# Output product of the biased layers split six and two, and the written-out order replaced

## The chip, the cores and the metric

One core of one Trainium2 chip runs the whole program. The metric is device time in microseconds (us) of one execution; the kernel before was timed in three runs.

## The reference, cut to what matters

Eight sequences (B = 8) of 512 tokens (T), width 256 (D), go through four layers, each with a layer norm ahead of it and a residual sum behind it:

```
x = x + attn_a(layernorm(x))     # l = 0: causal attention, 16 heads of 16, rotary positions
x = x + ffn(layernorm(x))        # l = 1: gate picks the top 256 of 512 tokens, attention among them
x = x + attn_b(layernorm(x))     # l = 2: attention, 16 heads of 64, learned relative bias
x = x + ffn(layernorm(x))        # l = 3: as l = 1
```

The change is in attn_b. Its last lines are, for each sequence:

```
attn = softmax(q @ k.T * 64**-0.5 + bias)
out = (attn @ v).transpose(0, 2, 1, 3).reshape(b, t, 16 * 64)
return out @ w_out.T                      # (512, 1024) by (1024, 256)
```

## The kernel before

**Steps.** The program is cut into steps `Step(kind, s, l, n, q)`: `s` is the sequence, `l` the layer, `n` and `q` count parts. Kinds that begin with `c_` belong to the causal layer, `f_` to the gated layers, `b_` to the biased layer. A step owns one or more of the eight PSUM banks (`UNITS`, with the engine that empties each), some matmuls on TensorE (PE), and the work behind them on VectorE (DVE), ScalarE (ACT), GpSimd (POOL) and the SP queue.

**The biased layer** handles heads in eight pairs `n`. For a pair: `b_k`, `b_q`, `b_v` project (each 1 bank); `b_row` (4 for a pair, one for each 128 tokens) makes scores of both heads in two banks, to which DVE adds the bias and takes maxima, ACT the exponentials; `b_nrm` divides on POOL; `b_tr` turns the rows around on PE and ACT copies them out; `b_val` (4 parts into one bank) multiplies by the values, and behind its last part DVE copies the bank to `OTb[:, n, :]` (line 1561). When the pairs are done, `b_y` multiplies by `wob`: `b_y(0, .)` for tokens 0 to 255 and `b_y(1, .)` for tokens 256 to 511, each in two parts `q` that add up in one bank: pairs 0 to 3, then pairs 4 to 7, 16 matmuls a part (line 1603). Behind `q = 1` DVE adds the bank to `x`, takes the moments for the next layer norm, and SP stores the rows.

**Where the steps of a kind run in the array.** Most kinds use all 128 rows and columns of PE. `c_p1`, `c_p2`, `f_p1`, `f_p2` (scores with heads of 16) use 32 rows, four heads at once; `b_row` uses 64 rows; `b_val` 64 columns; `c_va`, `c_vb`, `f_va`, `f_vb` 32 columns. The kernel's planner names these groups in `TILES`.

**Order.** Every engine walks one list, `plan.order`, and takes from it what is its own; waits are on semaphores whose counts follow from the list. The list comes from `in_order`: of all steps whose predecessors are listed, the one with the lowest `turn` goes next.

```
def turn(x):
    row, cycle = stage(x)
    return PLACE[row, x.kind][x.n * SEVERAL.get(x.kind, 1) + x.q] + CYCLE * cycle
```

`PLACE` is a table written out by hand or by a search, with the rows `first`, `first0`, `first1` (start), `cycle` and `cycle3` (six cycles that repeat for sequences 1 to 6, `CYCLE = 2820` apart), `last`, `last1`, `last2` (end). In one cycle the biased layer of sequence s runs among the causal layer and the first gated layer of s+1 and the last gated layer of s-1. `causal_steps`, `ffn_steps` and `biased_steps` list for each step what it needs and what it has to follow. `in_order` also keeps a clock of its own from the costs in `WORK`, with which it hands out banks; where that clock sees PE wait long enough, PE is given dummy transposes of the identity (line 1623).

**Steps of the last gated layer that the prediction follows.** `f_ln` (norm and gate logits), `f_row`, `f_rank` (the rank of each token: PE, then DVE writes `pick`, line 1507), `f_idx` (the token numbers, which need `pick`), `f_get` (POOL fetches the chosen rows by an indirect DMA, line 1214), `f_turn` (PE turns them around, line 1730), `f_k`, `f_q`, `f_v`, four `f_p1` (scores, DVE takes maxima, line 1533), `f_m`, four `f_p2` (scores again, less the maxima; ACT takes exponentials, line 1318), `f_va`, `f_vb`, `f_sc`, `f_add`.

Of the kernel before, what the change touches and what calls it, by code (L numbers as in the profile page):

```python
# [211 lines left out]
def wait_for(x, y):  # L212
# [52 lines left out]
    ("cycle", "f_k"): [170],
    ("cycle", "f_ln"): [-107],
    ("cycle", "f_m"): [365, 436],
    ("cycle", "f_o"): [569],
    ("cycle", "f_p1"): [320, -294, 345, 356],
    ("cycle", "f_p2"): [380, 425, 396, 262],  # L270
    ("cycle", "f_part"): [-4486],
    ("cycle", "f_q"): [184],
    ("cycle", "f_rank"): [40],
    ("cycle", "f_row"): [-1],
    ("cycle", "f_rq"): [-408],
    ("cycle", "f_spread"): [94],
    ("cycle", "f_v"): [219],
    ("cycle", "f_va"): [462, 518],
    ("cycle", "f_vb"): [-753, 405],
# [14 lines left out]
    ("cycle3", "f_q"): [5074],
    ("cycle3", "f_rank"): [4768],
    ("cycle3", "f_row"): [3336],
    ("cycle3", "f_rq"): [-1587],
    ("cycle3", "f_sc"): [5430],
# [1 line left out]
    ("cycle3", "f_v"): [5084],  # L300
    ("cycle3", "f_va"): [5264, 5321],
    ("cycle3", "f_vb"): [1319, 2872],
    ("cycle3", "f_xq"): [5131],
    ("first", "b_k"): [1394, 819, 1448, 733, 2071, 2459, 2798, 2934],
    ("first", "b_ln"): [1262],
    ("first", "b_nrm"): [1675, 401, 1780, -186, 1853, 324, 1822, 1309, 1850, 1318, 2266, 740, 2121, 1561, 2466, 2454,
        2590, 2321, 2692, 839, 2622, 1876, 2813, 2022, 2534, 3050, 3092, 3092, 2734, 2438, 3412, 3380],
    ("first", "b_q"): [292, 1680, 1268, 1633, 1493, 2254, 2809, 822],
    ("first", "b_row"): [1647, 1319, 1588, 563, 1806, 699, 882, 795, 2047, 1253, 1700, 1970, -80, -674, 2388, 2207,
        2680, 872, 2421, 2044, 2206, 2207, 2887, 2223, 2683, 3072, 2821, 3056, 1550, 2977, 3152, 3113],  # L310
    ("first", "b_tr"): [1760, 1445, 1875, 1948, 1118, 1745, 1969, 1940, 2270, 2311, 2340, 533, 2512, 1426, 923, 2494,
        2828, 2729, 2877, 2796, 2895, 2428, 2970, 3039, 3149, 3038, 3380, 3330, 3138, 3401, 3380, 3401],
# [9 lines left out]
    ("first0", "c_k"): [42, 95],
    ("first0", "c_ln"): [-178],
    ("first0", "c_m"): [400, 563],
    ("first0", "c_p1"): [238, 237, -199, 284, -197, -1423, -1423, 323, 252, 428, 323, 275],
    ("first0", "c_p2"): [292, -1395, 390, -1165, 310, 402, 399, 632, 284, -1207, 710, -954],
    ("first0", "c_q"): [30, 44],
    ("first0", "c_rq"): [-1391, 276],
    ("first0", "c_v"): [199, 145],
    ("first0", "c_va"): [529, 274, -486, 682, 724, 622],  # L330
    ("first0", "c_vb"): [585, 401, 607, 794, 720, 320],
    ("first0", "c_xq"): [111, 195],
    ("first0", "c_xt"): [17286],
    ("first0", "c_y"): [820, 273],
    ("first0", "f_gate"): [850],
    ("first0", "f_gather"): [1043],
    ("first0", "f_hk"): [752],
    ("first0", "f_hm"): [674, 1321],
    ("first0", "f_k"): [905],
    ("first0", "f_ln"): [840],  # L340
    ("first0", "f_m"): [1234, 1332],
    ("first0", "f_o"): [1437],
    ("first0", "f_p1"): [1153, 1192, 1270, 1240],
    ("first0", "f_p2"): [1293, 1250, 927, 660],
    ("first0", "f_part"): [887],
    ("first0", "f_q"): [819],
    ("first0", "f_rank"): [985],
    ("first0", "f_row"): [900],
    ("first0", "f_rq"): [-1182],
    ("first0", "f_spread"): [1430],  # L350
    ("first0", "f_v"): [1134],
    ("first0", "f_va"): [1338, 883],
    ("first0", "f_vb"): [1293, 1410],
    ("first0", "f_xq"): [1093],
    ("first0", "f_y"): [1457, 886],
    ("first1", "c_dk"): [408, 735],
    ("first1", "c_dq"): [351, 565],
    ("first1", "c_hk"): [429, 722],
    ("first1", "c_hm"): [854, 838],
    ("first1", "c_k"): [188, 278],  # L360
# [1565 lines left out]
```

How the kernel before makes its waits and increments, by code:

```python
            def at_least(engine, s, value):  # L1060
                if value > reached.get((id(engine), s.num), 0):
                    reached[id(engine), s.num] = value
                    engine.wait_ge(s, value)
# [32 lines left out]
                @block.sync  # L1097
# [10 lines left out]
                        sp.dma_start(dst[:], src).then_inc(w_rest, 16)  # L1108
                    for i in range(2):
                        sp.dma_start(wb[:, i], w_b[i]).then_inc(wb_loaded[i], 16)
                        sp.dma_start(band[:, i], band_in[i]).then_inc(band_loaded[i], 16)
                    load_x(sp, 2)
                    for now in plan.order:
                        kind, s, l, n, q = now
                        m = memory(now)
                        k = PAIRS * s + n
                        if kind == "f_vb" and l == 1 and n == 1 and 1 <= s < B - 1:
                            sp.wait_ge(heads_done, plan.after("heads", now, now))
                            load_rope(sp, s + 1)
                        if kind == "b_row" and q == NT - 1 and k + 2 < pairs:
                            sp.wait_ge(dve_read, plan.unit(now, now, "o2"))
                            sp.dma_start(band[:, k % 2], band_in[(k + 2) % PAIRS]).then_inc(band_loaded[k % 2], 16)
                        if kind == "b_v" and k + 2 < pairs:
                            sp.wait_ge(act_full, plan.unit(now, now))
                            sp.dma_start(wb[:, k % 2], w_b[(k + 2) % PAIRS]).then_inc(wb_loaded[k % 2], 16)
```

## Time and profile before

| | |
|---|---|
| median of three runs | 2005.87 us (2005.8 to 2006.48) |
| the profiled execution | 2006.36 us, its span 2004.6 us |
| PE busy | 1950.8 us, 97% of the span |
| DVE busy | 1486.9 us, 74% |
| ACT busy | 1152.3 us, 57% |
| POOL busy | 714.4 us, 36% |

Busy time of PE includes the dummy transposes and the filling and emptying of the array between matmuls of different shape. The chain that ended last is PE for 80% and DVE for 11% of its length.

### The profile page before, as it was taken

The numbers are of one execution on the slowest core, as the hardware profiler recorded it, in microseconds if no ns is written. First come the engines' busy times: TensorE is split into PE (matmuls) and PEld (weight loads), VectorE is DVE, ScalarE is ACT, GpSimd is POOL, SyncE is SP. The second block draws the span as 40 slices with busy tenths as digits, with TensorE's granted clock in tenths as the row PEclk, the third lists the DMA queues.
The fourth block names the chain that finished last, engine by engine and source line by source line (L and its number), as shares of the span: only waits on it lengthen the run. The fifth ranks groups of instructions, "written<-read, shape, count | busy, mean of one in ns | idle before, by whom it ended". The sixth has DMA issues, their size and how long they took to land.

```text
span 2004.6 us, 41582 instructions
## 1 busy us (share of the span) xinstructions
PE 1950.8 (97%) x15743; PEld 1244.9 (62%) x15743; DVE 1486.9 (74%) x4786; ACT 1152.3 (57%) x2588; POOL 714.4 (36%) x897
## 2 busy tenths in 40 slices
PE   8999999999999999999999999999999999999998
PEld 6666665656665666655666565665667556666566
DVE  8987666767879668877688677796877967856535
ACT  2554665475636766377553766457473675626753
POOL 5322324233433334333334333343333333404322
PEclk9999999999999999999999999999999999999999
DMA  4001211221201212112111122111220121212200
GB/s 171 2 2 43 72 64 45 66 69 44 76 23 62 75 41 69 38 46 98 41 56 46 36 90 59 38 47 52 80 68 26 62 69 33 76 34 81 71 12 12
DMA packets 37749, 110.02 MB, mean 55 GB/s; under 512 B 3696, under 2 KB 17648, under 8 KB 37424
## 3 DMA queue, kind: packets, MB, share of 16 engines
q1 hardware_dynamic: 34576, 103.43, 15.6%
q0 software_dynamic: 2976, 3.93, 1.1%
q8 instruction: 127, 2.08, 0.5%
q14 instruction: 70, 0.57, 0.1%
HBM read 97.39 MB, written 9.96 MB: 54 GB/s over the span
## 4 chain that ended last, share of the span: by engine, by line
PE 80%; DVE 11%; ACT 4%; issue 2%; DMA 2%; POOL 1%; POOLq 0%; DVEq 0%; ACTq 0%
PE ps L1036 24%; PE ps L1845 11%; PE ps L1837 10%; PE ps L1855 9%; PE ps L1603 9%; DVE peaks L1533 4%; PE ps L1797 3%; DVE ps L1448 3%; PE ps L1700 3%; PE ps L1686 3%; PE ps L1785 2%; ACT PTc L1294 2%; PE ps L1662 2%; DMA xg<-kept,tokens 2%; PE ps L1763 1%
## 5 line engine op out<-in xcount | busy, mean ns | idle before, releaser
L1228 POOL TENSOR_SCALAR probs<-probs,rtotal 128x512 f32<-128x512 f32 x512 | 359.2, 734 | 483.4 <-DVE rtotal L1559 483.4
L1338 ACT ACTIVATE probs<-probs,peak 128x512 f32<-128x512 f32 x512 | 365.0, 714 | 194.7 <-DVE peak L1555 194.6
L1550 DVE CUSTOM_DVE_ANT_0 probs<-ps,band 128x512 f32<-128x512 f32 x512 | 332.6, 687 | 60.8 <-PE ps L1837 60.7
L1347 ACT ACTIVATE PT<-ps 128x512 f32<-128x512 f32 x512 | 265.7, 621 | 48.8 <-PE ps L1845 48.0
L1845 PE MATMUL ps<-ident,probs 128*128 128x128 f32 x2048 | 250.3, 274 | 3.7 <-DVE peaks L1448 3.1
L1845 PEld LDWEIGHTS ps<-ident,probs 128*128 128x128 f32 x2048 | 225.8, 141 | 45.0 <-issue 34.1
L1448 DVE CUSTOM_DVE_ANT_0 ps<-ps,later 128x512 f32<-128x512 f32 (+3 forms) x512 | 232.8, 525 | 19.7 <-PE ps L1662 19.2
L1837 PE MATMUL ps<-KT,QT 64*128 64x512 f32 x1024 | 244.3, 608 | 0.0
L1855 PE MATMUL ps<-PT,Vb 128*64 128x512 f32 x1024 | 241.1, 602 | 0.0
L1036 PE MATMUL ps<-xnT,wb 128*128 128x512 f32 x512 | 234.7, 599 | 1.3 <-ACT xnT L1257 0.6
L1294 ACT ACTIVATE PTc<-ps 128x384 f32<-128x384 f32 (+1 forms) x384 | 168.0, 552 | 61.1 <-PE ps L1686 59.8
L1533 DVE TENSOR_REDUCE peaks<-ps 128x2 f32<-128x512 f32 x256 | 157.0, 682 | 26.0 <-PE ps L1763 26.0
L1036 PEld LDWEIGHTS ps<-xnT,wb 128*128 128x128 f32 x512 | 93.2, 190 | 109.5 <-issue 99.3
L1837 PEld LDWEIGHTS ps<-KT,QT 64*128 64x128 f32 x1024 | 97.6, 186 | 92.8 <-issue 71.1
L1318 ACT ACTIVATE PTf<-ps 128x512 f32<-128x512 f32 x256 | 130.2, 652 | 43.7 <-PE ps L1785 43.7
L1855 PEld LDWEIGHTS ps<-PT,Vb 128*64 128x64 f32 x1024 | 64.8, 136 | 123.3 <-issue 99.1
L1207 POOL TENSOR_SCALAR_AFFINE_SELECT PTc<-PTc 128x512 f32<-128x512 f32 x128 | 81.4, 648 | 159.3 <-ACT PTc L1294 159.3
L1036 PEld LDWEIGHTS ps<-wb,xnT 128*128 128x128 f32 x1024 | 120.6, 192 | 20.6 <-issue 9.2
L1036 PE MATMUL ps<-wb,xnT 128*128 128x128 f32 x1024 | 128.0, 279 | 0.0
L1176 POOL TENSOR_TENSOR rstd<-veps,pow_half 128x2 f32<-128x2 f32 x64 | 49.3, 800 | 185.8 <-DVE veps L1369 185.3
L1603 PE MATMUL ps<-wob,OTb 128*128 128x256 f32 x512 | 114.2, 380 | 0.5 <-DVE peaks L1448 0.5
L1603 PEld LDWEIGHTS ps<-wob,OTb 128*128 128x128 f32 x512 | 96.1, 190 | 16.9 <-issue 2.4
(191 smaller groups left out, 3213.9 us busy)
## 6 DMA issues: line engine op xcount, KB each, us to landing
band<-in_band SPq DMA_DIRECT2D x64, 896.0 KB, 4.6
wb<-in_w_b SPq DMA_DIRECT2D x64, 384.0 KB, 3.0
x<-in_x SPq DMA_DIRECT2D x16, 256.0 KB, 4.7
out<-x SPq DMA_DIRECT2D x16, 256.0 KB, 2.2
kept<-xn SPq DMA_DIRECT2D x7, 512.0 KB, 5.0
cos<-in_cos SPq DMA_DIRECT2D x8, 256.0 KB, 2.7
sin<-in_sin SPq DMA_DIRECT2D x8, 256.0 KB, 3.1
wob<-in_wo_b SPq DMA_DIRECT2D x1, 1024.0 KB, 8.5
```

The costliest lines, as they stand in the source:

```text
L1036: last = nc.tensor.matmul(o, w, r, start=(i == 0), stop=(i == len(pairs) - 1))
L1228: last = g.tensor_scalar(unit, unit, rtotal[:, r % 8, e:e + 1], 1.0, ALU.mult, ALU.mult)
L1294: a.activation(pt_c(m, q)[:, h], bank(now, name)[:, 0:w], ACT.Exp, scale=float(DH) ** -0.5).then_inc(act_read, 1)
L1338: last = a.activation(unit, unit, ACT.Exp, bias=peak[:, r % 8, e:e + 1], accum_out=total[:, r % 8, e:e + 1])
L1347: a.activation(PT[:, k % 2, e, :, tile_of(q)], bank(now, name).rearrange("p (k n) -> p k n", k=NT), ACT.Copy).then_inc(act_read, 1)
L1448: last = v.tensor_tensor_reduce(out=scores, in0=scores, in1=later[:, NT * P - w:NT * P], scale=1.0, scalar=-3e38, op0=ALU.add, op1=ALU.max ...
L1533: v.tensor_reduce(places[:, h:h + 1].rearrange("p h t -> p (h t)"), bank(now, name).rearrange("p (t n) -> p t n", t=NS), AXIS.X, ALU.max). ...
L1550: v.tensor_tensor_reduce(out=probs[:, (r + LENT) % ROWS_HELD, e, :], in0=bank(now, name), in1=band[:, k % 2, e, lo:lo + T], scale=1.0, sca ...
L1603: last = te.matmul(o[:, j * D:(j + 1) * D], w, r, start=(k == 0 and j == 0), stop=(k == count - 1 and j == 1))
L1837: full(te.matmul(bank(now, name), QT2[half(e), k % 2, tile_of(q)], KT2[half(e), k % 2, :], start=True, stop=True), now, name)
L1845: last = te.transpose(bank(now, name)[:, tile_of(t)], probs[:, (r + LENT) % ROWS_HELD, e, tile_of(t)], ident[:])
L1855: last = te.matmul(o[half(e), :], Vb[:, k % 3, q, half(e)], PT[:, k % 2, e, q, :], start=(q == 0), stop=(q == NT - 1))
```

## The change

`b_y(i, 0)` now covers pairs 0 to 5 (24 matmuls) and needs only `b_val(5, 3)`; `b_y(i, 1)` covers pairs 6 and 7 (8 matmuls) and needs `b_val(7, 3)`. `b_y(1, 0)` has to follow `b_y(0, 0)`, no longer `b_y(0, 1)`, so two banks can hold unfinished sums at once. The whole of `PLACE` is replaced. The number of matmuls, copies and DMAs stays as it was. Of the table, the rows that the prediction speaks of:

```diff
+EARLY = 6
...
-    ("b_y", 0): [("pe", 3.453)],
-    ("b_y", 1): [("pe", 3.453), ("dve", 1.82)],
+    ("b_y", 0): [("pe", 5.178)],
+    ("b_y", 1): [("pe", 1.726), ("dve", 1.82)],
...
-    ("cycle", "b_k"): [705, 371, 880, 1163, 1851, 1946, 2325, 2599],
+    ("cycle", "b_k"): [680, 324, 944, 1217, 1767, 1917, 2407, 2492],
...
-    ("cycle", "b_row"): [797, 240, 389, 852, 556, 223, 1085, 678, 461, 1561, 370, 799, 436, 156, 1053, 656, 2002, -379,
-        2034, -831, -4407, -4407, 2630, -3472, 2058, 2492, 2719, 2449, 25, 2864, 2979, 1287],
+    ("cycle", "b_row"): [719, 315, 743, 873, 397, 677, -343, 831, -617, 1519, 397, -8286, -343, 357, -617, -4332, 2022,
+        -1730, -3347, -1208, -969, -1061, 2747, 299, 373, 1445, 2895, -10069, -1992, -6438, 1482, -4890],
...
-    ("cycle", "b_val"): [1285, 933, 1257, 1291, 1606, 1294, -4709, 566, 2096, 932, -1826, -1276, -1727, 2269, 2312,
-        2413, 2797, 1084, -992, 2150, 1084, 2843, -1819, -1434, 3084, 3173, 3187, 3219, 3318, 3279, -2665, 3199],
+    ("cycle", "b_val"): [1346, -799, 1127, 1408, 1523, 677, -912, -355, 2085, 1184, 1705, 1989, 2275, -2222, 2346,
+        2627, 2859, 134, 821, 2122, -2502, -5970, 2847, -398, 3072, 3126, 3215, 3236, 3277, 3248, 3144, 3217],
...
-    ("cycle", "b_y"): [3358, 3464, 3216, 3524],
+    ("cycle", "b_y"): [3319, 3496, 3464, 2205],
...
-    ("cycle", "c_p2"): [-1587, -1533, -1478, -5079, -1563, -2142, -1719, -2488, -1315, -2424, -3589, -2489],
+    ("cycle", "c_p2"): [-1560, -1440, -1409, -2482, -1415, -3237, -1554, -4375, -1306, -3732, -1326, -4787],
...
-    ("cycle", "c_va"): [-1437, -2456, -2311, -1309, -2240, -2142],
-    ("cycle", "c_vb"): [-1419, -2487, -2365, -1207, -2689, -1327],
+    ("cycle", "c_va"): [-1369, -1875, -1618, -1293, -1602, -2316],
+    ("cycle", "c_vb"): [-1356, -1555, -2508, -1191, -3734, -3734],
...
-    ("cycle", "c_y"): [-891, -2551],
+    ("cycle", "c_y"): [-910, -742],
...
-    ("cycle3", "f_idx"): [4845],
+    ("cycle3", "f_idx"): [4832],
...
-    ("cycle3", "f_p1"): [-1588, 5132, 5193, 5166],
-    ("cycle3", "f_p2"): [5233, 5235, 1046, 3115],
+    ("cycle3", "f_p1"): [4755, 5223, 5428, 5277],
+    ("cycle3", "f_p2"): [5470, 5551, -538, 1906],
...
-    ("cycle3", "f_turn"): [4942],
+    ("cycle3", "f_turn"): [2718],
...
-    ("first", "b_y"): [3623, 3378, 3846, 3222],
+    ("first", "b_y"): [3307, 3536, 3965, 1099],
...
-    ("last", "b_y"): [22109, 22093, 22093, 22093],
+    ("last", "b_y"): [21720, 12486, 19500, 17309],
...
-    ("last2", "f_m"): [21795, 22137],
-    ("last2", "f_p2"): [22087, 22158, 22194, 22093],
-    ("last2", "f_va"): [22116, 22278],
-    ("last2", "f_vb"): [22210, 22093],
+    ("last2", "f_m"): [21795, 21886],
+    ("last2", "f_p2"): [22149, 17298, 17249, 12484],
+    ("last2", "f_va"): [16776, 23572],
+    ("last2", "f_vb"): [20247, 14673],
...
@@ biased_steps
     for i in range(2):
-        out += [(b("y", i, 0), [b("val", PAIRS - 1, 3)], [b("y", 0, 1)] * i), (b("y", i, 1), [b("val", PAIRS - 1, 3)], [b("y", i, 0)])]
+        out += [(b("y", i, 0), [b("val", EARLY - 1, 3)], [b("y", 0, 0)] * i),
+                (b("y", i, 1), [b("val", PAIRS - 1, 3)], [b("y", i, 0)] + [b("y", 0, 1)] * i)]
     return out
...
@@ TensorE, kind b_y
+                            read(now, Step("b_val", s, l, (EARLY, PAIRS)[q] - 1, 3))
                             if q == 0:
-                                read(now, Step("b_val", s, l, PAIRS - 1, 3))
                                 room(now)
                             last = sums(o, lambda j, g: (OTb[:, g, tile_of(2 * n + j)], wob[:, g, :]), PAIRS,
-                                        range(PAIRS // 2 * q, PAIRS // 2 * (q + 1)))
+                                        range(EARLY * q, (EARLY, PAIRS)[q]))
```

## Rows read from the trace of the kernel before

**Rows 1.** Busy time by stretch: us, then each engine's busy us (instructions), PE clock, DMA.
```profile
0.00:100.00 100.00, 92.58 (x873) 63.27 (x874) 91.25 (x324) 36.50 (x72) 49.04 (x63) 0.98 0.24 87
...
827.60:1068.20 240.60, 235.92 (x1906) 148.03 (x1905) 186.18 (x599) 143.92 (x323) 88.90 (x111) 1.00 0.18 56
...
1947.50:2004.60 57.10, 47.55 (x585) 37.18 (x584) 34.95 (x99) 21.29 (x44) 12.05 (x9) 0.96 0.10 15
```

**Rows 2.** Line 1561, the copy to OTb: instructions, and who waited for it.
```profile
L1561 DVE COPY OTb<-ps x64: 668/683/693, 218.0 to 1932.7; 128x512 f32<-128x512 f32 x64
...
PEld ps L1837: 0.4, 1
```

**Rows 3.** Timeline of PE and DVE around the first output product of one cycle.
```profile
1042.62 3.65 PE L1855 MATMUL ps<-PT,Vb 128*64 128x512 f32 x16
...
1046.41 0.68 DVE L1561 COPY OTb<-ps 128x512 f32<-128x512 f32 x1
...
1049.00 3.62 PE L1603 MATMUL ps<-wob,OTb 128*128 128x256 f32 x16
```

**Rows 4.** Chain of waits in one cycle, PE pieces: start us, us, line, instructions.
```profile
832.00 5.15 PE ps L1036 x12
...
850.27 5.35 PE ps L1036 x12
...
907.72 4.49 PE ps L1837 x20
912.21 3.58 PE ps L1855 x16
...
929.45 3.46 PE ps L1603 x16
932.91 3.91 PE ps L1036 x28
936.82 2.68 PE ps L1845 x24
...
959.25 1.01 PE ps L1855 x4
```

**Rows 5.** Timeline of PE where it waited in the same cycle.
```profile
906.81 0.39 PE L1686 MATMUL ps<-X,LO 32*128 32x256 f32 x4 [0.27 <-ACT PTc L1294]
...
952.46 0.66 PE L1730 MATMUL ps<-ident,xg 128*128 128x128 f32 x4 [1.10 <-DMA xg<-kept,tokens]
...
973.91 0.39 PE L1785 MATMUL ps<-gX,gLO 32*128 32x256 f32 x4 [0.84 <-DVE peaks L1533]
```

**Rows 6.** Timeline of DVE and POOL from the gate row to the fetch.
```profile
936.22 0.68 DVE L1576 TENSOR_TENSOR x<-x,ps 128x512 f32<-128x512 f32 x1
...
938.22 0.68 DVE L1539 TENSOR_SCALAR QT<-ps 128x512 f32<-128x512 f32 x1
...
939.00 1.56 DVE L1507 TENSOR_SCALAR pick<-slot_row,smalls 128x256 fp32r<-128x256 bf16 x4
...
942.20 1.03 PE L1036 MATMUL ps<-marks,pick 128*128 128x4 f32 x8
...
945.62 1.21 POOL L1214 DMA_INDIRECT xg<-kept,tokens  x1 [0.17 <-issue]
```

**Rows 7.** Chain of waits at the end.
```profile
1932.66 0.91 PE ps L1785 x22
...
1947.59 1.00 PE ps L1797 x16
...
1954.39 0.45 PE ps L1713 x4
```

**Rows 8.** Timeline of the end, ACT and PE.
```profile
1959.49 0.18 PE L1036 MATMUL ps<-ones,tie1b 128*128 128x1 bf16 x1
...
1962.11 0.39 PE L1036 MATMUL ps<-pick,xn_hi 128*128 128x256 f32 x1
...
1984.55 2.07 ACT L1318 ACTIVATE PTf<-ps 128x512 f32<-128x512 f32 x4 [1.07 <-PE ps L1785]
```

More of the change, by code:

```diff
@@ L265 @@
[L265 to L279, printed above, removed]
@@ L294 @@
[L294 to L298, printed above, removed]
-    ("cycle3", "f_turn"): [4942],
[L300 to L312, printed above, removed]
@@ L322 @@
[L322 to L345, printed above, removed]
@@ L346 @@
[L346 to L360, printed above, removed]
@@ L371 @@
-    ("first1", "c_xt"): [47],
-    ("first1", "c_y"): [1588, 811],
-    ("first1", "f_gate"): [1546],
-    ("first1", "f_gather"): [1828],
-    ("first1", "f_hk"): [1806],
-    ("first1", "f_hm"): [2268, 2320],
-    ("first1", "f_k"): [1904],
-    ("first1", "f_ln"): [1440],
-    ("first1", "f_m"): [2328, 2439],
-    ("first1", "f_o"): [2779],
-    ("first1", "f_p1"): [1980, 2182, 2310, 2260],
-    ("first1", "f_p2"): [2387, 2464, 2465, 2540],
-    ("first1", "f_part"): [777],
-    ("first1", "f_q"): [1912],
@@ L414 @@
-    ("last1", "f_gather"): [22300],
-    ("last1", "f_hk"): [21414],
-    ("last1", "f_hm"): [22072, 12176],
-    ("last1", "f_idx"): [22344],
-    ("last1", "f_k"): [20275],
-    ("last1", "f_ln"): [22184],
-    ("last1", "f_m"): [22241, 22500],
-    ("last1", "f_mk"): [22291],
-    ("last1", "f_p1"): [12177, 21877, 22107, 22396],
-    ("last1", "f_p2"): [20273, 22421, 15242, 15241],
-    ("last1", "f_part"): [22107],
-    ("last1", "f_q"): [21172],
-    ("last1", "f_rank"): [22222],
-    ("last1", "f_row"): [22108],
@@ new lines @@
+    ("cycle", "f_k"): [180],
+    ("cycle", "f_ln"): [-8682],
+    ("cycle", "f_m"): [318, 418],
+    ("cycle", "f_o"): [531],
+    ("cycle", "f_p1"): [254, -5308, 302, 325],
+    ("cycle", "f_p2"): [400, 417, 421, -158],
+    ("cycle", "f_part"): [-2517],
+    ("cycle", "f_q"): [214],
+    ("cycle", "f_rank"): [73],
+    ("cycle", "f_row"): [28],
+    ("cycle", "f_rq"): [-8946],
+    ("cycle", "f_spread"): [-5605],
+    ("cycle", "f_v"): [220],
+    ("cycle", "f_va"): [422, 475],
+    ("cycle", "f_vb"): [-82, -326],
@@ new lines @@
+    ("cycle", "f_xq"): [251],
+    ("cycle", "f_y"): [622, 399],
+    ("cycle3", "f_add"): [-826],
+    ("cycle3", "f_gate"): [-1011],
+    ("cycle3", "f_get"): [1264],
+    ("cycle3", "f_hk"): [2643],
+    ("cycle3", "f_hm"): [2416, -2627],
+    ("cycle3", "f_idx"): [4832],
+    ("cycle3", "f_k"): [4916],
+    ("cycle3", "f_ln"): [4575],
+    ("cycle3", "f_m"): [5325, 5502],
+    ("cycle3", "f_mk"): [4015],
+    ("cycle3", "f_p1"): [4755, 5223, 5428, 5277],
+    ("cycle3", "f_p2"): [5470, 5551, -538, 1906],
@@ new lines @@
+    ("cycle3", "f_q"): [5006],
+    ("cycle3", "f_rank"): [4756],
+    ("cycle3", "f_row"): [4592],
+    ("cycle3", "f_rq"): [4407],
+    ("cycle3", "f_sc"): [5730],
+    ("cycle3", "f_turn"): [2718],
+    ("cycle3", "f_v"): [5014],
+    ("cycle3", "f_va"): [5583, 5607],
+    ("cycle3", "f_vb"): [2300, -1325],
+    ("cycle3", "f_xq"): [5109],
+    ("first", "b_k"): [-414, 1449, -698, -1068, 2242, -1306, -71, 1933],
+    ("first", "b_ln"): [-1240],
+    ("first", "b_nrm"): [1426, -243, -246, 563, -1269, 1614, 1234, -4514, -557, 493, -3384, -562, 1666, -535, -4567,
+        1446, 1734, -1268, 1051, 1419, 578, 1908, -2242, 106, 1235, 2651, -37, -5429, -1021, -3384, 2572, 2927],
@@ new lines @@
+    ("first0", "c_vb"): [613, -2597, -281, 760, -2403, 90],
+    ("first0", "c_xq"): [1, 314],
+    ("first0", "c_xt"): [-551],
+    ("first0", "c_y"): [829, -2471],
+    ("first0", "f_gate"): [-2813],
+    ("first0", "f_gather"): [1037],
+    ("first0", "f_hk"): [-2475],
+    ("first0", "f_hm"): [376, -174],
+    ("first0", "f_k"): [81],
+    ("first0", "f_ln"): [888],
+    ("first0", "f_m"): [1317, 1582],
+    ("first0", "f_o"): [4633],
+    ("first0", "f_p1"): [1156, 1192, 1203, 1288],
+    ("first0", "f_p2"): [408, 1312, -1530, -50],
@@ new lines @@
+    ("first0", "f_part"): [932],
+    ("first0", "f_q"): [-607],
+    ("first0", "f_rank"): [974],
+    ("first0", "f_row"): [935],
+    ("first0", "f_rq"): [-948],
+    ("first0", "f_spread"): [2014],
+    ("first0", "f_v"): [693],
+    ("first0", "f_va"): [1777, 2162],
+    ("first0", "f_vb"): [-737, 495],
+    ("first0", "f_xq"): [520],
+    ("first0", "f_y"): [1767, 2205],
+    ("first1", "c_dk"): [406, 515],
+    ("first1", "c_dq"): [393, 484],
+    ("first1", "c_hk"): [-603, 801],
+    ("first1", "c_hm"): [-1731, 580],
@@ new lines @@
+    ("first1", "c_xq"): [-447, 445],
+    ("first1", "c_xt"): [-310],
+    ("first1", "c_y"): [5297, -95],
+    ("first1", "f_gate"): [1037],
+    ("first1", "f_gather"): [1759],
+    ("first1", "f_hk"): [377],
+    ("first1", "f_hm"): [-1, 2507],
+    ("first1", "f_k"): [1895],
+    ("first1", "f_ln"): [1027],
+    ("first1", "f_m"): [2299, -899],
+    ("first1", "f_o"): [3091],
+    ("first1", "f_p1"): [2131, 2237, 2411, 2355],
+    ("first1", "f_p2"): [2547, 2659, -553, 2238],
+    ("first1", "f_part"): [-428],
@@ new lines @@
+    ("first1", "f_q"): [-2771],
+    ("first1", "f_rank"): [1507],
+    ("first1", "f_row"): [1398],
+    ("first1", "f_rq"): [-27],
+    ("first1", "f_spread"): [2771],
+    ("first1", "f_v"): [2656],
+    ("first1", "f_va"): [2831, 2937],
+    ("first1", "f_vb"): [2478, -4564],
+    ("first1", "f_xq"): [-505],
+    ("first1", "f_y"): [3305, -4115],
+    ("last", "b_k"): [20105, 20157, 20117, 20139, 20153, 20287, 21428, 15177],
+    ("last", "b_ln"): [19961],
+    ("last", "b_nrm"): [20637, 20572, 19895, 20103, 20751, 20244, 20158, 20102, 19811, 19943, 20043, 19624, 21427,
+        20262, 20106, 20137, 17229, 20137, 20647, 19686, 20744, 20113, 19573, 11768, 20118, 19826, 20241, 19701, 19506,
+        12486, 20075, 17299],
@@ new lines @@
+    ("last1", "f_hk"): [16728],
+    ("last1", "f_hm"): [17249, 19497],
+    ("last1", "f_idx"): [26532],
+    ("last1", "f_k"): [17189],
+    ("last1", "f_ln"): [21910],
+    ("last1", "f_m"): [17307, 20037],
+    ("last1", "f_mk"): [12484],
+    ("last1", "f_p1"): [12484, 17157, 17307, 19454],
+    ("last1", "f_p2"): [12484, 19834, 20010, 14093],
+    ("last1", "f_part"): [17297],
+    ("last1", "f_q"): [17249],
+    ("last1", "f_rank"): [23144],
+    ("last1", "f_row"): [17235],
+    ("last1", "f_rq"): [14730],
@@ new lines @@
+    ("last1", "f_sc"): [17249],
+    ("last1", "f_v"): [19951],
+    ("last1", "f_va"): [20010, 17307],
+    ("last1", "f_vb"): [21053, 18270],
+    ("last1", "f_xq"): [28331],
+    ("last2", "f_add"): [12485],
+    ("last2", "f_gate"): [20108],
+    ("last2", "f_get"): [20533],
+    ("last2", "f_hk"): [20388],
+    ("last2", "f_hm"): [16045, 20264],
+    ("last2", "f_idx"): [20397],
+    ("last2", "f_k"): [20644],
+    ("last2", "f_ln"): [20107],
+    ("last2", "f_m"): [21795, 21886],
+    ("last2", "f_mk"): [20104],
@@ L456 @@
+    ("last2", "f_p1"): [20149, 21679, 20258, 21465],
+    ("last2", "f_p2"): [22149, 17298, 17249, 12484],
+    ("last2", "f_q"): [20750],
+    ("last2", "f_rank"): [20211],
+    ("last2", "f_row"): [19879],
+    ("last2", "f_rq"): [20137],
+    ("last2", "f_sc"): [27562],
+    ("last2", "f_turn"): [20150],
+    ("last2", "f_v"): [20815],
+    ("last2", "f_va"): [16776, 23572],
+    ("last2", "f_vb"): [20247, 14673],
+    ("last2", "f_xq"): [21133],
 }
```

179 lines of the change are left out of this document (73 added, 106 removed).

## The prediction

> **What bounds the kernel now.** I read the page's busy times first, then busy time by stretch, the waits, the chain of waits, and the timelines of the places that came out of these. TensorE (PE) is the bound: in one of the six repeating cycles, 240.6 us long, it is busy 235.92 us, and the granted clock is 1.00, the upper level of 2.4 GHz [rows 1]. DVE has 186.18 us of work in a cycle. Only the start differs: there DVE is busy 91.25 of the first 100 us. At the end, 57.1 us, nothing is full; it is a chain through all engines.
>
> So a change that leaves the number of matmuls alone can gain in a cycle in two ways: PE waits less, or PE loses less between matmuls of different shape. The second loss hides in the busy time, and the chain of waits shows it. The same 12 matmuls of 512 columns on line 1036 took 5.15 us behind others of full shape and 5.35 us behind the 64-row scores of `b_row` [rows 4]: entering the full shape cost 0.20. Four `b_val` matmuls (64 columns) took 1.01 us, 16 took 3.58 [rows 4]: 0.214 each, and 0.15 to enter. `b_row`'s 20, five steps, took 4.49; at 0.214 each that is 4.28, so 0.21 to enter. For the other two shapes (32 rows, 32 columns) I take `b_val`'s 0.15, the nearest.
>
> The Trainium skill ("TensorE: Matmul & The Clock Gate", Single matmul latency) puts what one matmul costs beyond its columns, when no neighbour hides it, at about 166 ns at the full clock. With that for each entry that goes, six a cycle, my estimate from the page is 1.0 us a cycle where the rows below give 1.12, and 1997 for the whole.
>
> **The change part by part.**
>
> *The early product itself: nothing.* What it is to spare is the wait of the first product for the last copy to `OTb`. Of the 64 copies not one held up a product: the only wait put down to them is 0.4 us of a weight load of `b_row` [rows 2]. In the cycle the last `b_val` begins at 1042.62, its copy starts at 1046.41 and takes 0.68, and the product starts at 1049.00, 1.9 us later [rows 3]; `f_va`, `f_vb` and `b_xt` or `c_xt` hide it. Without that cover it would cost under 1 us a cycle. And by the new `PLACE` the first product of a cycle (3319) still comes behind `b_val(7, .)` (3277 at most), so that it is not early.
>
> What the split adds: `b_y(0, 0)` and `b_y(1, 0)` now both hold a bank until the two short parts, for some 20 us. Between them stand only steps of one or two banks, 1.7 us of PE each, that DVE or ACT empties in 0.7 to 1.4 us. Below: nothing. Above: two waits of 0.7 (a copy of 512 columns [rows 6]), 1.4 us a cycle. I take 0.3, near the lower end, since six banks are left for one-bank steps. The two final sums on DVE and their two stores on SP now come 1.7 us apart instead of 7. Who needs them is the next norm, in the cycle tens of us later: nothing.
>
> *The order.* I sorted one cycle by the new table, each time the lowest place among the steps that are ready. Up to the last `c_p2` of the third group it is the old order. Then three stretches differ. F is the full shape, A 32 rows, R 64 rows (`b_row`), V 64 columns (`b_val`), H 32 columns.
>
> 1. From the third group's last `c_p2`: A H A H A H A R V H F R F becomes A R V H A H A F R H F.
> 2. From the rows of pair 4 to the first `f_p1` of the last gated layer: F R F R V F V F A becomes F R F V F V A; `b_row(4, 0)` to `(5, 1)` come as one run of six, and `c_y(1)` moves behind them.
> 3. Behind the first `f_p2` of that layer: F H A H A F H F R F R V F V F R F R F becomes F A R F H A H A F H F V F R F R F.
>
> That is two entries less in each: in 1 one H and one A, in 2 one R and one F, in 3 one R, one V and one F less and one A more. Together 2 x 0.21 + 2 x 0.20 + 0.15 (V) + 0.15 (H) + 0 (A) = 1.12 us a cycle. With 0.10 for each of the six it would be 0.6, with 0.21 1.3.
>
> *Waits of PE that lie in these stretches* [rows 5]: 0.27 us for exponentials of `c_p2`, 1.10 at `f_turn` for the fetched rows, 0.84 at `f_p2` for maxima on DVE; 2.21 us a cycle. The first should go: `b_row` and `b_val`, 8.1 us [rows 4], now stand where the exponentials pile up. The third too: 1.7 us of `b_tr` is put between the `f_p1`, so that DVE gains on PE. The second moves:
>
> - `f_idx` now comes sooner behind `f_row`: half of `c_y` (1.73), then `b_k`, `b_q`, `f_rank` (3.91), then three `b_tr` (2.68) [rows 4], 8.32 us. It needs `pick`, which DVE finished at 940.56, 11.1 us behind `f_row`'s end at 929.45 [rows 4, 6]. With `c_y(1)` moved away DVE has one block less (936.22 to 938.22, 2.0 us [rows 6]): 9.1. So PE waits 0.8 us at `f_idx`.
> - Then `f_turn`. From the start of `f_get` on POOL (945.62) to the transposes (952.46) it took 6.8 us [rows 5, 6]. `f_idx` itself ends at 943.23 [rows 6]; 2.4 us went between it and the fetch, on rows that DVE had queued and a `b_nrm` that POOL had ahead of the fetch. In the new order the fetch stands ahead of both, so I take 0.8. That is 1.0 + 0.8 + 6.8 = 8.6 us from `f_idx`'s start, and PE has 1.0 + six `b_row` (5.4) + half of `c_y` (1.7) = 8.1: 0.5 us of wait. If the 2.4 stays, 2.1.
>
> So waits go from 2.21 to 1.3, minus 0.9 a cycle. Bounds: all gone, minus 2.2; none gone, 0.8 added at `f_idx` and 2.1 instead of 1.1 at `f_turn`, plus 1.8.
>
> A cycle: -1.1 - 0.9 + 0.3 = -1.7 us; six: -10.2.
>
> *The end.* Before the last `b_y`, `f_p2` (0.91 [rows 7]) and `f_m` (two transposes, about 0.4) of the last gated layer's first half go behind the products, so these end 1.3 us sooner. But four `f_p2`, not two, with `f_va` and `f_vb` now stand between the last `f_row` and `f_rank`, paced by ACT: 0.5 + 0.5 + 2.07 for a step's exponentials [rows 8], then 1.0 + 0.9 + 1.0 + 0.9, 6.9 us, where it was 1954.39 to 1959.49, 5.1 [rows 7, 8]. `f_gather` comes 1.7 later likewise. Net +0.4; bounds -1.3 and +1.7.
>
> *The start.* Its order changes too, but DVE is nearly full there and its work is the same: 0, with bounds of 4 us each way, half of the 8.75 us in which DVE is idle in the first 100.
>
> Sum against the profiled execution: 2006.36 - 10.2 + 0.4 = 1996.6 us. It lies 0.49 over the median of the runs, so 1996.1 as a median: -0.5%.
>
> **The rivals.** A measurement of this kernel can tell about 0.2%, 4 us, from no change.
>
> *The change does not do what it says, and the order nothing more (within 0.2%).* The early product has no wait to remove, as shown. If of the new order only the shape entries count and at the three places new waits of 0.8 us eat most of them, a cycle gives -0.3 and the whole 2004. For it: at 97% busy every us that PE saves at one place tends to show up as a wait for DVE at the next. Against it: DVE has 54 us free in a cycle. 0.18.
>
> *Slower, through the fetch and the banks.* Place: `f_idx` and `f_turn`. PE takes its list in order, so behind a late `f_idx` stand six `b_row`, and behind a late `f_turn` the `b_val` and `f_k`, `f_q`, `f_v`; DVE gets 9 us of `b_row` work at once. With waits of 0.8 and 2.1 there, the others kept (1.1), 1.4 for held banks and the entries at 1.1 less, a cycle costs 0.8 + 1.0 + 1.4 - 1.1 = 2.1 more: 2018 us. It decides from 0.7 us a cycle on, that is, when the new waits exceed the saved ones by 1.8. For it: rows 5 show that PE already waits at that fetch. 0.08.
>
> The Trainium skill ("Perfetto Trace Analysis", Optimization Strategy) says that the same gap, come again and again on an engine that should be full, can mean that no PSUM is left for the next tile. By that rule the held banks would cost their upper bound; the waits of rows 5 are put down to other things.
>
> *The start gains too.* If 4 us go there and the waits all vanish (-3.3 a cycle), it is 2005.87 - 19.8 - 4 + 0.4 = 1982. Everything would have to fit; 0.05.
>
> **How the numbers follow.** The forecast, 1990 to 2001.8, has 0.69. The time is its centre, 1996.1. Faster by over 0.2%: 0.69 + 0.05 = 0.74; within: 0.18; slower: 0.08. The range 1988 to 2005 leaves out the slower case, the upper half of "within" and most of the large gain, 0.2 in all.
>
> **What would show it.** A cycle near 238.9 us, same cadence in all six. In the list of lines no change in counts but the dummy transposes. PE's wait at line 1730 near 0.5 us a cycle, a new one of 0.8 at line 1036 for `pick`, none of 0.84 at line 1785. `b_row` in a run of six. Line 1603 in parts of 24 and 8 with no wait for line 1561, as before. The prediction is wrong if PE shows waits for emptied banks between 1603's parts, if the cycle is not shorter than 240 us, or if the time goes or comes outside the cycles.

## The result: 2% slower, and the profile after

The changed kernel takes 2045.32 us (median of 4 runs, 2045.07 to 2045.95), the kernel before 2006.17 on the same chip: a ratio of 1.0195, 95% interval 1.0177 to 1.0212. Forecast were 1996.1 and a range of 1988 to 2005. The profiled execution took 2045.07 us, its span is 2043.2.

The same views as before, first the busy time by stretch: one cycle, and then five short stretches of the cycle before it.

```profile
1086.30:1333.09 246.79, 235.88 (x1905) 148.91 (x1905) 185.71 (x599) 143.93 (x324) 88.83 (x110) 0.98 0.17 54
...
1014.00:1020.00 6.00, 6.00 (x46) 5.60 (x44) 4.59 (x18) 6.00 (x18) 2.09 (x4) 1.00 0.42 153
1020.00:1022.00 2.00, 1.22 (x6) 0.30 (x4) 1.45 (x5) 0.02 (x1) 2.00 (x4) 1.00 0.00 0
1022.00:1029.50 7.50, 0.00 (x0) 0.00 (x0) 1.26 (x5) 0.18 (x1) 4.49 (x4) 0.74 0.31 35
1029.50:1037.00 7.50, 7.03 (x18) 4.65 (x19) 2.68 (x9) 5.28 (x13) 0.00 (x0) 0.58 0.32 110
1037.00:1045.00 8.00, 8.00 (x79) 6.55 (x77) 5.10 (x12) 6.19 (x11) 6.19 (x6) 1.00 0.03 12
```

The cycle is 246.79 us long instead of 240.60, and PE is as busy as before: 235.88 against 235.92 [rows 1]. What grew is PE's idle time, from 4.7 to 10.9 us, and most of the growth lies in one place. From 1022.00 to 1029.50 no engine but GpSimd (POOL) does much, and PE nothing at all. Behind the gap the granted clock is 0.58 for 7.5 us, mostly the lower level of 1.2 GHz, and only then 1.00 again.

The waits of PE name the place, and it comes once in each of the six cycles:

```profile
PE ps L1840 <- ACT xgT L1317: 52.5, 6, 8.8
...
PE ps L1733 <- DMA xg<-kept,tokens: 1.2, 1, 1.2
```

No such line stood among the waits before. PE's waits at the fetch, 7.4 us in the kernel before, of which [rows 5] shows one, are down to 1.2. The timeline of the same stretch (start, us, engine, line; in brackets the idle time ahead and what ended it):

```profile
1014.06 2.00 PE L1606 MATMUL ps<-wof,OTf 128*128 128x256 f32 x8
...
1017.91 5.36 POOL L1231 TENSOR_SCALAR probs<-probs,rtotal 128x512 f32<-128x512 f32 x8 [11.54 <-DVE rtotal L1562]
...
1019.21 0.81 ACT L1310 ACTIVATE of<-ps,gates_sel 128x256 f32<-128x256 f32 x2
...
1020.09 1.13 PE L1840 MATMUL ps<-KT,QT 64*128 64x512 f32 x4
...
1023.44 1.67 POOL L1224 DMA_INDIRECT out<-of,tokens  x1 [0.18 <-issue]
...
1025.42 1.56 POOL L1224 DMA_INDIRECT out<-of,tokens  x1 [0.31 <-issue]
...
1029.32 0.60 ACT L1317 ACTIVATE xgT<-ps 128x512 f32<-128x512 f32 x1 [9.29 <-DMA out<-of,tokens]
...
1029.97 2.08 PE L1840 MATMUL ps<-KT,QT 64*128 64x512 f32 x4 [8.75 <-ACT xgT L1317]
```

Read it from the top. `f_sc`, the output product of the last gated layer's chosen tokens (here of sequence s-1), is computed at 1014.06. ScalarE (ACT) copies it to `of`, times the gate, only at 1019.21, behind the exponentials of four `b_row`. POOL starts the scatter-add that `f_add` issues (two indirect DMAs that add the rows of `of` to `out`) at 1023.44, behind the `b_nrm` of those rows. It lands at 1029.3. The next thing in ACT's queue is the copy for `f_gather` of sequence s+1 (PE picks the chosen tokens of the first gated layer), whose turned tokens `xgT` lie in the columns (10752 on) from which the scatter-add still reads `of`. So ACT waits for the landing, 9.29 us. ACT is in order, so the copies of the transposed probabilities and the exponentials behind it wait too. In the kernel's plan the next `b_row` of PE takes the PSUM bank in which the product of `f_gather` lies, and this copy is what empties it; so PE stops there, and is released by the copy. At the low clock this `b_row` then took 2.08 us, where the one at 1020.09 took 1.13. The chain of waits goes the same way:

```profile
1021.25 2.02 POOL probs L1231 x3
1023.27 0.18 issue
1023.44 1.67 POOL out L1224
1025.11 0.31 issue
1025.42 3.82 DMA out<-of,tokens
...
1029.32 0.61 ACT xgT L1317
1029.92 0.04 issue
1029.97 2.08 PE ps L1840 x4
```

In the kernel before, the same steps of the same cycle stood like this:

```profile
986.51 1.93 PE L1603 MATMUL ps<-wof,OTf 128*128 128x256 f32 x8
...
988.48 0.84 ACT L1307 ACTIVATE of<-ps,gates_sel 128x256 f32<-128x256 f32 x2 [1.01 <-PE ps L1603]
...
990.24 1.65 POOL L1221 DMA_INDIRECT out<-of,tokens  x1 [22.13 <-ACT of L1307]
...
992.20 1.57 POOL L1221 DMA_INDIRECT out<-of,tokens  x1 [0.31 <-issue]
...
1015.35 0.57 ACT L1314 ACTIVATE xgT<-ps 128x512 f32<-128x512 f32 x1
```

There `f_sc` came 28.8 us ahead of ACT's copy for `f_gather`, here 15.3, and all of it is needed: 5.2 until ACT has worked through its queue, 4.2 until POOL has, 5.9 for the scatter-add. The new table moves `f_sc` from place 5430 to 5730 (in the cycle: from 2610 to 2910), directly ahead of `f_spread` and `f_gather`.

### The profile page after: what moved, and what is told of

Same layout as the page of the kernel before. It is cut to its first block, busy times and chain, and to the rows that moved or that the text cites. A ratio compares the mean times of both kernels' runs of the same rounds, so it can differ in the third digit from the quotient of the medians.

```text
span 2043.2 us, 41581 instructions
## 1 busy us (share of the span) xinstructions
PE 1948.6 (95%) x15728; PEld 1247.4 (61%) x15728; DVE 1489.8 (73%) x4786; ACT 1152.9 (56%) x2588; POOL 714.4 (35%) x897
## 3 DMA queue, kind: packets, MB, share of 16 engines
q8 instruction: 127, 2.08, 0.4%
## 4 chain that ended last, share of the span: by engine, by line
PE 85%; DVE 6%; ACT 2%; POOL 2%; issue 1%; DMA 1%; ACTq 0%; POOLq 0%; DVEq 0%
PE ps L1039 25%; PE ps L1858 11%; PE ps L1840 11%; PE ps L1848 11%; PE ps L1606 8%; PE ps L1703 3%; PE ps L1689 3%; PE ps L1800 3%; PE ps L1788 3%; PE ps L1665 2%; PE ps L1766 2%; DVE ps L1451 2%; DVE probs L1553 2%; POOL probs L1231 1%; DMA out<-of,tokens 1%
## 5 line engine op out<-in xcount | busy, mean ns | idle before, releaser
L1231 POOL TENSOR_SCALAR probs<-probs,rtotal 128x512 f32<-128x512 f32 x512 | 353.1, 709 | 613.3 <-DVE rtotal L1562 613.1
L1840 PE MATMUL ps<-KT,QT 64*128 64x512 f32 x1024 | 246.0, 616 | 52.5 <-ACT xgT L1317 52.5
```

The lines of the kernel that those rows point to most:

```text
L1231: last = g.tensor_scalar(unit, unit, rtotal[:, r % 8, e:e + 1], 1.0, ALU.mult, ALU.mult)
L1840: full(te.matmul(bank(now, name), QT2[half(e), k % 2, tile_of(q)], KT2[half(e), k % 2, :], start=True, stop=True), now, name)
```

## Experiments

Theory 1: this wait and the low clock behind it are the whole loss, and the rest of the change gains. Theory 2: the split product and the banks that it holds cost the time. Theory 3: another stretch of the new order does.

**own_memory: the changed kernel, `of` in other columns.** Order and split stay.

```
-   part("of", 10752, [P, NS, D])
+   part("of", 11264, [P, NS, D])
    kind in ("f_gather", "f_turn"), ACT:
-   at_least(act, out_added, 32 * plan.after("added", old, now))
    the same at_least goes to the next users of columns 11264 on:
    f_o on DVE, f_get on POOL, c_m and f_sc on ACT
```

> The changed kernel with its order and its split kept; the output of f_sc gets columns 11264 to 11775 of the side memory instead of 10752 to 11263, so that it no longer lies where the next gated layer's turned tokens are written, and ScalarE no longer waits for the scatter-add at f_gather and f_turn (later writers of columns 11264 on, a long way behind, wait instead). Theory 1 (the added time is ScalarE's in-order wait for the scatter-add, 8.75 us in each of six cycles, and the lower clock of TensorE that follows it, some 3 us a cycle): 2045 less 52.5 and up to 20, so 1972 to 1993. Theory 2 (the split product and the banks that it holds cost the time): stays at 2043 to 2047. Theory 3 (another stretch of the new order, such as the one run of six score rows, costs it): 2035 to 2046.

Measured: 1978.89 us, ratio to the kernel before 0.9861 (0.9846 to 0.9876). PE's wait for `xgT` is gone, and nothing took its place:

```profile
1052.61:1288.66 236.05, 233.89 (x1905) 148.22 (x1905) 186.27 (x599) 143.77 (x324) 88.80 (x110) 1.00 0.18 57
```

```profile
992.10 1.99 PE L1615 MATMUL ps<-wof,OTf 128*128 128x256 f32 x8
...
997.25 0.82 ACT L1319 ACTIVATE of<-ps,gates_sel 128x256 f32<-128x256 f32 x2
...
997.96 0.59 ACT L1323 ACTIVATE xgT<-ps 128x512 f32<-128x512 f32 x1
...
998.13 1.99 PE L1849 MATMUL ps<-KT,QT 64*128 64x512 f32 x8
...
1001.48 1.67 POOL L1227 DMA_INDIRECT out<-of,tokens  x1 [0.18 <-issue]
```

ACT copies `xgT` straight behind `of`, 3.5 us before the scatter-add is even started, and PE goes on. Theory 1 as forecast. The cycle is 10.7 us shorter than in the changed kernel: 8.75 of idle time and 1.99 of busy time (235.88 to 233.89), which is what the low clock had cost there. Over the whole program PE's busy time is 14.9 us shorter (1948.6 to 1933.7 us), some 2.5 a cycle, at a mean granted clock of 0.999 instead of 0.984. With `own_memory_split4` (below) this is the fastest version of the study.

**before_own_memory: the same edit on the kernel before**, as a control.

> The kernel before with the other memory for the output of f_sc (columns 11264 to 11775), and without ScalarE's wait for the scatter-add at f_gather and f_turn; order and split as before. A control for the run own_memory. Theory 1 (the wait had been covered in the kernel before by the 27 us between f_sc and f_gather): no change, 2005 to 2008. If the new memory itself, or a wait hidden in the kernel before, were worth something: below 2003.

Measured: 2007.12 us, ratio 1.0003 (0.9994 to 1.0012). The memory alone is worth nothing; in the old order the scatter-add was covered.

**before_sc_late: the kernel before with `f_sc` moved alone**, by 24 of PE's steps (the text put down before the run says 25).

```
-   ("cycle3", "f_sc"): [5430]
+   ("cycle3", "f_sc"): [5733]
```

> The kernel before with one step moved: f_sc stands 25 steps of TensorE later, directly ahead of f_spread, as in the changed kernel; nothing else of TensorE's order changes, and the output product is not split anew. Theory 1 (ScalarE's wait for the scatter-add): the wait appears here as well, 6 x (6 to 11 us) and the low clock behind it, so 2040 to 2080. Theories 2 and 3: within 3 us of the kernel before, 2003 to 2009.

Measured: 2061.41 us, ratio 1.0270 (1.0255 to 1.0286).

```profile
PE ps L1036 <- ACT xgT L1314: 47.8, 6, 8.5
...
1043.31 3.40 PE L1036 MATMUL ps<-xgT,wkf 128*128 128x256 f32 x8 [7.63 <-ACT xgT L1314]
```

One step of 218 in a cycle, moved by itself, costs 54.6 us without anything else of the change. In the profiled execution 47.8 are this wait, and PE's busy time rose by 9.2 us (1950.8 to 1960.0 us) at a mean granted clock of 0.985 instead of 0.997. Theories 2 and 3 had 2003 to 2009 here. PE stops at another step than in the changed kernel: at `f_k`, which reads `xgT` itself, and not for a bank.

**sc_early, sc_ahead_of_rank, sc_between_values: the changed kernel with `f_sc` moved alone**, by 15, 5 and 9 of PE's steps; the two that had followed it keep their place.

```
-   ("cycle3", "f_sc"): [5730]
+   5615 (sc_early), 5712 (sc_ahead_of_rank), 5683 (sc_between_values)
-   ("cycle", "f_gather"): [-2315], ("cycle", "f_spread"): [-5605]
+   [91], [90]
```

> The changed kernel with one step moved: f_sc stands 15 steps of TensorE earlier, ahead of f_row instead of ahead of f_spread, in each of six cycles; no other step of TensorE's order changes, and there are as many entries of the array's shapes. Theory 1 (ScalarE's wait for the scatter-add): the scatter-add is started some 10 to 12 us earlier, the wait of 8.75 us falls to 0 to 2, so 1972 to 2000. Theory 2 (split product and held banks): 2043 to 2047. Theory 3 (another stretch of the new order): 2035 to 2046.

> The changed kernel with f_sc moved by 5 steps of TensorE alone, from directly ahead of f_spread to directly ahead of f_rank (four b_row lie between); as many entries of the array's shapes, no new dummy transposes; memory and ScalarE's wait as in the changed kernel. Theory 1: f_sc comes 2.6 us earlier on TensorE, but ScalarE's copies of it and the scatter-add then stand ahead of the eight exponentials and of four rows' b_nrm on GpSimd, behind which they stood in the changed kernel; the scatter-add lands some 8 us earlier and the wait of 8.75 us falls to 0 to 3 a cycle: 1979 to 2002. If only TensorE's 2.6 us count: the wait falls to 6, 2020 to 2035. Theories 2 and 3: 2040 to 2047.

> The changed kernel with f_sc moved by 9 steps of TensorE, to between the head products of pairs 4 and 5; two more entries of the array's shapes in each of six cycles (93), no new dummy transposes; memory and ScalarE's wait as in the changed kernel. Theory 1: the scatter-add lands before f_gather is read; what is left is the price of 12 entries at the 0.15 us that six_more_entries gave: 1979 plus 1.8, 1979 to 1984. Theories 2 and 3: 2040 to 2047.

Measured, in this order: 1998.25 (1997.29 to 1998.41), 1998.94 (1995.27 to 2003.12) and 1987.35 us (1986.83 to 1988.44); theories 2 and 3 had 2035 or more for each. In the order of distance, PE's wait for `xgT` over six cycles falls with it: 52.5 us in the changed kernel, 13.5 at 5 steps, 3.3 at 9, 2.4 at 15. The run `sc_ahead_of_rank` shows how fine the margin is. Two of its cycles, ACT's copy, the scatter-add ahead of it, and a load of `band` that SP issues in between:

```profile
1477.22 1.67 POOL L1224 DMA_INDIRECT out<-of,tokens  x1 [7.22 <-ACT of L1310]
1479.19 1.56 POOL L1224 DMA_INDIRECT out<-of,tokens  x1 [0.31 <-issue]
...
1479.98 0.33 SPq L1125 DMA_DIRECT2D band<-in_band  x1
...
1488.74 0.60 ACT L1317 ACTIVATE xgT<-ps 128x512 f32<-128x512 f32 x1 [4.08 <-DMA out<-of,tokens]
...
1721.12 1.67 POOL L1224 DMA_INDIRECT out<-of,tokens  x1 [7.22 <-ACT of L1310]
1723.09 1.56 POOL L1224 DMA_INDIRECT out<-of,tokens  x1 [0.30 <-issue]
...
1723.88 0.33 SPq L1125 DMA_DIRECT2D band<-in_band  x1
...
1729.37 0.60 ACT L1317 ACTIVATE xgT<-ps 128x512 f32<-128x512 f32 x1 [0.81 <-DMA out<-of,tokens]
```

The same two stretches, from the second issue to ACT's copy, and one of the changed kernel, with the DMA share and GB/s at the end of the line:

```profile
1479.19:1488.74 9.55, 5.64 (x42) 4.38 (x40) 7.38 (x26) 5.45 (x16) 6.92 (x9) 0.97 0.53 125
1723.09:1729.37 6.28, 5.64 (x42) 4.38 (x40) 4.89 (x21) 5.46 (x16) 3.75 (x5) 1.00 0.78 188
...
1025.42:1029.32 3.90, 0.00 (x0) 0.00 (x0) 0.00 (x0) 0.00 (x1) 1.55 (x1) 0.53 0.60 67
```

From the second issue to ACT's copy it is 9.6 us in one cycle and 6.3 in the other, so the wait comes and goes from cycle to cycle, which may be the wide spread of this kernel's times. In the changed kernel it is 3.9 us in each of the six cycles, and no other load runs beside the scatter-add there. In `sc_ahead_of_rank` (6.3 to 9.6 us) and `before_sc_late` (6.2 to 7.0) the 896 KB load of `band` runs beside it in all six. So the landing was late where that load ran beside it; no run moves the load alone, and why one cycle takes 9.6 us and another 6.3 stays open.

`sc_between_values` came out 3 us above its range. Its 0.55 us of wait a cycle (3.3) was not expected, and 12 entries at 0.18 (below) are 2.1; 3 us stay unexplained. `sc_early` is inside its range, but its 19 us over `own_memory` are not the wait for `xgT`: there PE finds the heads of `f_vb` not ready. The planner foresees this and puts 13 dummy transposes ahead of `f_sc`.

**sc_early_no_dummies: the same without those transposes** (a dummy is left out where the step is `f_sc` inside the cycles).

> The run sc_early without the 13 dummy transposes that the planner puts ahead of f_sc in each of six cycles where its model sees a wait of 2.8 us for the heads of f_vb. If that wait is real, as the wait ahead of c_p1 was in split_no_dummies: 1996 to 2000 as in sc_early, with the wait for OTf in place of the transposes. If the transposes are the cost: 1980 to 1987.

Measured: 2002.01 us, ratio 0.9974 (0.9964 to 0.9984).

```profile
PE ps L1606 <- DVE OTf L1485: 13.5, 7, 2.2
```

The wait is real; the transposes only fill it. Without them it is 13.5 us where `sc_early` had 4.1, and 3.8 us more in all, above the range: the mean granted clock is 0.996 here and 0.999 there. So `f_sc` has a window. Too early it waits for `f_vb`'s heads, too late its scatter-add holds up ACT.

**split_alone and split_no_dummies: the split in the old order.** `EARLY = 6`, the new costs in the planner's list and the new code of `b_y`, with the old `PLACE`; one place of `b_y` is changed so that the order of all steps is the old one. The second leaves out the dummy transposes ahead of `c_p1` inside the cycles.

```
-   ("cycle", "b_y"): [3358, 3464, 3216, 3524]
+   ("cycle", "b_y"): [3358, 3464, 3465, 3524]
    split_no_dummies only:
-   if kind != "c_xt" and wait > (0.4 if ends else 1):
+   if kind != "c_xt" and wait > (0.4 if ends else 1) and (ends or kind != "c_p1"):
```

> The kernel before, its order of steps kept whole, with the output product cut behind six pairs instead of four: the first part takes 12 of a half's 16 products and waits for pair 5, the second 4 and waits for pair 7. Theory 1 and theory 3: within 1 us of the kernel before (2005 to 2007), since the parts stand where they stood and the same products run. Theory 2 (the split costs): 2012 or more. The prediction's own term for the banks that a split half holds longer (0.3 us a cycle) belongs to the new order and would not show here.

> The run split_alone without the 8 dummy transposes that the planner newly puts ahead of c_p1 in each of five cycles (its modelled wait there rises to 1.74 us, above its limit of 1; on the chip no such wait is recorded). If these 40 transposes are the 7.5 us of split_alone (0.19 us each): the split alone is then 2005 to 2008. If the split product and its banks cost the time: it stays at 2012 to 2016.

Measured: 2014.27 us, ratio 1.0038 (1.0024 to 1.0052), and 2013.82, ratio 1.0037 (1.0024 to 1.0051). Theories 1 and 3 had 2005 to 2007 for the first, theory 2 had 2012 or more: in the old order the split does cost time. My explanation by the transposes fell with the second: without them the wait that the planner foresaw is there, once in each of five cycles:

```profile
1053.01 5.35 PE L1605 MATMUL ps<-wob,OTb 128*128 128x256 f32 x24
...
1080.64 4.97 POOL L1202 TENSOR_TENSOR LO<-LOf,HI 128x512 fp32r<-128x512 f32 x4 [4.51 <-ACT HI L1282]
...
1083.25 0.33 PE L1664 MATMUL ps<-LO,X 32*128 32x128 f32 x4 [1.41 <-issue]
```

Nothing in the list of waits points to the banks; the trace shows what is late. The first part of the product is 24 matmuls instead of 16, 5.35 us instead of 3.62 [rows 3], and stands ahead of `f_o`, `c_q` and `c_k`. From these goes a chain through DVE, ACT and POOL, which makes the halves `LO` for the first `c_p1`. From the start of the product to POOL's first half it is 25.92 us in the kernel before (1049.00 to 1074.92) and 27.63 here (1053.01 to 1080.64). The chain starts 1.7 us later, the products that would have covered it now come earlier, and PE waits 1.41 us at `c_p1`. The profile names no engine for this wait ("issue"); that it is for POOL's halves is read from the times, and no run removes it. Five times 1.41 is 7.1 of the 7.8 us.

**own_memory_split4: the split taken back in the new order.** `own_memory` with `EARLY = 4` and the old costs of `b_y`; every step of PE stands where it stood.

> The run own_memory (new order, no wait for the scatter-add) with the output product cut behind four pairs again, every step of TensorE where it stood, and without dummy transposes ahead of b_xt that the planner's costs would add. If the early product is worth nothing in itself, as the prediction has it, because its first part stands behind the last head product in either kernel: 1978 to 1981. If the first part of 12 products is itself what the rest of the gain comes from: 1985 or more.

Measured: 1978.64 us, ratio 0.9862 (0.9847 to 0.9877), against 1978.89 with six pairs. What the change is named for is worth nothing in the new order; the whole gain of `own_memory` is the order's.

**six_more_entries: `own_memory` with 36 more changes of shape.**

```
-   b_q(1) 767, b_v(1) 438, b_v(5) 2211, b_val(3, 1) -2222, b_tr(5, 3) 2854, b_val(4, 2) 821
+   b_q(1) 740, b_v(1) 745, b_v(5) 2280, b_val(3, 1) 2281, b_tr(5, 3) 2862, b_val(4, 2) 2865
```

> The run own_memory with four steps of TensorE moved by one to five places (b_q and b_v of pair 1 into the run of b_row, b_v of pair 5 into the run of b_val, b_tr of the last row of pair 5 into the run of b_val), so that the array changes shape six times more in each of six cycles, 97 times as in the kernel before instead of 91; no product is added. By the prediction's price (0.187 us an entry, 1.12 us a cycle): 1979 plus 6.7, 1984 to 1988. If the rest of the gain of the new order (4.5 us a cycle, of which 2.3 us are waits that are gone) is entries alone, at 0.37 us each: 1990 to 1994. If entries cost nothing: 1978 to 1981.

Measured: 1984.16 us, ratio 0.9890 (0.9875 to 0.9905).

```profile
1055.97:1293.11 237.14, 234.95 (x1906) 147.90 (x1905) 186.25 (x599) 143.78 (x325) 88.82 (x110) 1.00 0.18 57
```

The cycle is 1.09 us longer than in `own_memory`, 1.06 of it busy time of PE: 0.18 us an entry in the profiled executions, and 0.15 by the medians, which are 5.3 us apart. So the prediction's price of 0.187 was right or a little high, and the rest of the gain is not entries alone. The Trainium skill ("TensorE: Matmul & The Clock Gate", Single matmul latency) puts what one matmul costs beyond its columns, when no neighbour hides it, at about 166 ns at the full clock; by that the 36 entries are 6.0 us, an estimate. This case agrees: the medians differ by 5.3 us, the profiled executions by 6.4.

## Why the prediction was wrong

**The step that failed** is the third string of the part on the order: F H A H A F H F R F R V F V F R F R F becomes F A R F H A H A F H F V F R F R F. The string is right; the shapes follow each other in PE's order as I had them. But in it I only counted shapes. `f_sc` moved inside it from one full-shape run to another: 25 steps of PE had stood between it and `f_gather`, now one does. For that I wrote nothing down, since no entry changed, and so the wait behind it stands in the sum as nothing. I did not follow what it issues: two copies on ACT, `f_add`'s two scatter-adds on POOL, and the wait of ACT for their landing at the next `f_gather`. That wait was no row of any view of the kernel before, where it was covered. It stood in the code (`out_added`) and in the overlap of `of` and `xgT` at column 10752. It cost 8.75 us a cycle, 52.5 in six, and 14.9 of PE's busy time at the low clock behind it, 67.4 together; `own_memory`, where it is gone, is 66.4 us faster (67.2 in the profiled executions), and `before_sc_late` shows it by itself in the old order. Of the prediction's own signs of being wrong one came: the cycle is not shorter than 240 us.

**The terms that I had**, six cycles each, against `own_memory`, which has the order without that wait. A cycle went from 240.60 to 236.05, by 4.55 us; forecast was 1.7.

- *Entries*: six fewer a cycle, priced at 1.12; at the measured 0.15 to 0.18 they are 0.9 to 1.1. Right.
- *Waits*: forecast minus 0.9, with new ones of 0.8 at `f_idx` and 0.5 at `f_turn`. PE's idle time fell from 4.68 to 2.16 us, by 2.5. Neither new wait came: `f_turn` follows `f_idx` by 8.15 us in the changed kernel (8.1 forecast), and the fetch is there, no more than 5.9 us behind POOL's start, where I had counted on 6.8. The bound "all gone, minus 2.2" was nearer than the value that I took.
- *Held banks*: forecast plus 0.3; nothing in the new order (`own_memory_split4`). In the old order the split costs 1.4 us in each of five cycles, by my reading through the chain to `c_p1`, which I had not seen.
- The rest, some 1.0 us a cycle, is busy time of PE that no run here assigns; its cause stays open.
- *Start and end*: forecast plus 0.4. The spans differ by 28.6 us (2004.6 and 1976.0), six cycles make 27.3, so minus 1.3.

The fetch in the changed kernel: `f_idx`, POOL's first issue, `f_turn`, which waits for nothing:

```profile
948.00 1.03 PE L1039 MATMUL ps<-marks,pick 128*128 128x4 f32 x8
...
950.29 1.22 POOL L1217 DMA_INDIRECT xg<-kept,tokens  x1 [3.62 <-DVE gates_sel L1526]
...
956.15 0.60 PE L1733 MATMUL ps<-ident,xg 128*128 128x128 f32 x4
```

**The early product** was judged rightly: nothing. In the changed kernel too, as in [rows 3], the last `b_val` begins first (at 1059.72), then its copy to `OTb` (1063.51), then the product (1066.10); no product waits for a copy.

**The rivals.** The slower one was priced at 2018, through `f_idx`, `f_turn` and held banks. Its sign came true by luck, by none of these. What I had left out of it was a transfer other than the fetch. Beside it I cited the Trainium skill ("Perfetto Trace Analysis", Optimization Strategy), that a gap which repeats on the full engine can mean that no PSUM is left. The trace agrees in part: PE stops 8.75 us in each of six cycles at `b_row` for a bank. But the bank is late since ACT, which empties it, is held up; in `before_sc_late` PE stops about as long at `f_k`, for the data. It took one edit of memory, not more banks, to end it.

## What to carry to other kernels

When an order changes, list for each moved step not only what it needs, but who waits for what it issues, and above all waits that have never been long enough to show: two tensors in one place of memory and a DMA between them are such a wait, and its cover is the distance in time. A written-out or searched order is only as good as the waits its cost list knows; here the list had the fetch but not the landing of the scatter-add, and the wait that it lacked cost 3% of the kernel. A wait on an in-order engine that empties PSUM soon stops TensorE: here ACT stood from 1020.0 on and PE from 1021.2.

## What the runs showed of the hardware

- A scatter-add of two indirect DMAs was slow to start and uneven to land: 1.67 and 1.56 us on POOL for the two. From the second issue to ACT's copy behind it, it took 3.9 us where no other load ran (the changed kernel), and 6.3 to 9.6 us, from cycle to cycle, where a load of 896 KB ran beside it (`sc_ahead_of_rank`).
- PE idle for 8.75 us came back at the lower clock: 0.58 granted over the next 7.5 us, 1.00 behind them, some 2.5 us of busy time in each cycle. Dummy transposes in a wait were worth 3.8 us over six waits of some 2 us (`sc_early` against `sc_early_no_dummies`).
